# First cross attention of a two-block decoder: whole-chunk exponentials from four score banks, one work bank, and query transfers moved behind a barrier

## The reference

```python
# x: (16, 56, 128); ctx: (16, 1500, 96)
# block 0: 16 heads of width 8
q, k, v = split(x @ w_qkv + b_qkv)                     # self attention over 56 rows
x = layer_norm(x + mha(q, k, v) @ w_so + b_so)
qc = x @ w_q + b_q                                     # cross attention: 56 queries,
kc = ctx @ w_k + b_k                                   # 1500 keys per batch element
vc = ctx @ w_v + b_v
x = layer_norm(x + mha(qc, kc, vc) @ w_co + b_co)      # mha: softmax(q k^T / sqrt(8)) v
x = layer_norm(x + mlp(x))                             # 128 -> 512 -> 512 -> 128, relu
# block 1: 16 heads of width 64, cross attention over the same ctx, residual
```

## The kernel before

| stretch, us | what is done |
|---|---|
| 0 to 56 | loads, self attention of block 0 |
| 56 to 80.5 | the *query block*: projection, layer norm, queries of the cross attention |
| 80.5 to 444 | the *cross block*: first cross attention, one batch element after the other |
| 444 to 558 | the MLP and the folded weights of block 1 |
| 558 to 1077 | second cross attention |

## Time and profile before

### The profile page before, as it was taken

One profiled execution on the slowest core, in us unless ns is written; L12 is line 12 of the kernel. 1 busy time (PEld: TensorE's weight loads), 2 busy tenths in 40 slices (PEclk: granted clock), 3 DMA queues, 4 the chain that ended last, 5 costly groups with the idle time before them and its releaser, 6 DMA issues. The chain is left out here.

```text
span 1076.9 us, 31227 instructions
## 1 busy us (share of the span) xinstructions
PE 995.5 (92%) x11876; PEld 718.2 (67%) x11876; DVE 721.9 (67%) x1369; ACT 559.2 (52%) x1107; POOL 413.9 (38%) x290
## 2 busy tenths in 40 slices
PE   6947999999999999697879999999999999999997
PEld 3633666666667666555337777777777777777786
DVE  5738787777877786204776667676776776767752
ACT  2622777677767776522434545444444444444542
POOL 5613223322332223020015645545555454455542
PEclk8976999999999999889799999999999999999998
DMA  3515666775677652300111012111011111102100
GB/s 105 145 26 141 183 169 177 183 190 161 172 182 187 174 152 48 101 1 1 41 40 48 32 58 61 57 39 54 28 51 56 58 51 42 54 23 58 36 4 3
DMA packets 90924, 91.34 MB, mean 85 GB/s; under 512 B 50882, under 2 KB 77716, under 8 KB 90868
## 3 DMA queue, kind: packets, MB, share of 16 engines
q1 hardware_dynamic: 90868, 90.56, 30.7%
HBM read 51.15 MB, written 22.18 MB: 68 GB/s over the span
## 5 line engine op out<-in xcount | busy, mean ns | idle before, releaser
L1451 ACT ACTIVATE P<-PS 125x448 f32<-125x448 f32 x384 | 207.1, 544 | 265.2 <-PE PS L1360 263.3
L1341 POOL TENSOR_TENSOR Pl<-P 125x896 f16<-125x896 f32 x128 | 230.2, 1803 | 236.8 <-ACT P L1451 236.8
L1087 DVE TENSOR_REDUCE m<-PS 128x1 f32<-128x500 f32 x336 | 220.6, 674 | 115.8 <-PE PS L1078 113.8
L988 DVE TENSOR_REDUCE m_part<-PS 128x1 f32<-128x500 f32 x336 | 213.1, 673 | 58.5 <-PE PS L891 56.5
L966 ACT ACTIVATE Pb<-PS 125x448 f32<-125x448 f32 x384 | 184.6, 546 | 30.0 <-PE PS L864 28.6
L1376 PE MATMUL PS<-cNh,P 125*128 125x97 f16 x1344 | 197.9, 208 | 0.1
L1378 PE MATMUL PS<-cNh,Pl 125*128 125x97 f16 x1344 | 197.4, 207 | 0.0
L1377 PE MATMUL PS<-cNl,P 125*128 125x96 f16 x1344 | 196.8, 206 | 0.0
L891 PE MATMUL PS<-KH,Qmx 128*128 128x500 f16 x336 | 130.5, 390 | 21.3 <-DVE m_part L988 9.5
L1377 PEld LDWEIGHTS PS<-cNl,P 125*128 125x128 bf16 x1344 | 131.8, 98 | 25.5
L1376 PEld LDWEIGHTS PS<-cNh,P 125*128 125x128 bf16 x1344 | 131.1, 98 | 15.8 <-issue 3.2
(11 more groups left out here) (174 smaller groups left out, 1446.8 us busy)
## 6 DMA issues: line engine op xcount, KB each, us to landing
Kst<-k_halves SPq DMA_DIRECT2D x144, 125.0 KB, 2.9
k_halves<-KH SPq DMA_DIRECT2D x16, 750.0 KB, 3.3
cx<-in_ctx SPq DMA_DIRECT2D x16, 562.5 KB
d_cx<-in_ctx SPq DMA_DIRECT2D x16, 562.5 KB
c_halves<-cHi SPq DMA_DIRECT2D x16, 288.0 KB, 2.9
c_halves<-cLo SPq DMA_DIRECT2D x16, 288.0 KB, 7.8
cTh<-c_halves SPq DMA_DIRECT2D x16, 288.0 KB, 3.0
cTl<-c_halves SPq DMA_DIRECT2D x16, 288.0 KB, 4.0
```

The lines of the kernel that those rows point to most:

```text
L988: nc.vector.tensor_reduce(m_part[:, t, part:part + 1], PS[:, 6 + k % 2, 0:SP], AX.X, ALU.max).then_inc(s_reduced, 1)
L1087: nc.vector.tensor_reduce(m21[:, t, part:part + 1], PS[:, S1[k % 2], 0:SP], AX.X, ALU.max).then_inc(n_red, 1)
L1341: nc.gpsimd.tensor_tensor(Pl[:, c % NP], P1[:, c % NP], high, ALU.subtract).then_inc(n_low_p, 1)
L1451: nc.scalar.activation(P1[:, c % NP, half * HALF:(half + 1) * HALF], PS[0:KC, u % 3, 0:HALF], ACT.Exp).then_inc(n_exp, 1)
```

## The change

Nothing in the arithmetic changes. The parts are these:

- *Scores and exponentials.* Four banks (0 to 3) instead of three; a chunk takes two neighbouring banks, and one instruction of 896 columns makes its exponential. The scores of chunk c wait once, for the exponential of chunk c-2.
- *One work bank.* Keys, values, output, attention and the turned maxima all use bank 5. The maxima move there from bank 7, so piece 1 no longer waits until they are laid; every other user now waits for its forerunner.
- *Keys at every second step.* `k_piece` and `keep_keys` come at steps 5, 7 and 9 instead of 3, 4 and 5, `split_keys` at 6, 8 and 10. Steps 8 and 9 now have 1 and 2 pieces instead of 2 and 1, so the last piece comes after the last keys of step 9.
- *Output* at steps 3 and 4 instead of 6, 7 and 8.
- *Context.* Loads are cut into two halves and go a body further ahead; `round_rows` comes at step 12 for element b+4, in the starting body at step 0 for element 2 and at step 12 for element 3; `turn_rows` goes ahead of `lay_keys`.
- *Query block.* `norm_root` comes ahead of `keep_values`, the three value pieces have a bank each, and the 12 query transfers are the first thing that SP does in the cross block.

The diff, cut to its core:

```diff
-        OB, WB, WB2, MB = 4, 5, 3, 7
-        K_BANK, V_BANK = (WB2, WB, WB2), WB2
+        OB, WB = 4, 5
+        M_AT = slice(128, 256)
+        K_BANK, V_BANK = WB, WB
+        SCORE_BANKS = 4
...
-        BESIDE = beside(EARLY, (2, 2, 2, 2, 1, 2, 1, 2, 2, 1, 0, 0, 0, 0))
+        BESIDE = beside(EARLY, (2, 2, 2, 2, 1, 2, 1, 2, 1, 2, 0, 0, 0, 0))
+        K_AT = {5: 0, 7: 1, 9: 2}
...
+            if in_loop:
+                sp.wait_ge(v_made, (n - 2) * 3)
+            for half in range(2):
+                if in_loop and half == 1:
+                    sp.wait_ge(cx_low, n - 2)
+                sp.dma_start(cx[:, slot, 6 * half:6 * half + 6], ctx_768[n].rearrange("(p c) d -> p c d", c=NC)[:, 6 * half:6 * half + 6]).then_inc(cx_in[slot], 16)
...
-            elif k == 1:
-                wait_for(pe, att_kept, n - 3)
+                wait_for(pe, att_kept, n - 2)
             else:
-                pe.wait_ge(k_split, n * 3 + 1)
+                pe.wait_ge(k_split, n * 3 + k)
...
-            @block.sync
-            def _(sp):
-                sp.wait_ge(a_high, 1)
-...
...
             def _(act):
+                norm_root(act, a_var, a_root)
                 for k in range(NSP):
-                    keep_values(act, -1, 1, k)
-                norm_root(act, a_var, a_root)
+                    keep_values(act, -1, 1, k, early=True)
...
+                for block_row in range(2):
+                    for g in range(G):
+                        sp.dma_start(Q16[32 * block_row:32 * block_row + 32, g, :], Qall[32 * g:32 * g + 32, :]).then_inc(q_in, 16)
+                for g in range(G):
+                    sp.dma_start(Q16[64:96, g, :], Qrest[32 * g:32 * g + 32, :]).then_inc(q_in, 16)
+                load_context(sp, -1, 1, 3)
+
                 def body(i, par):
-                    if inside(i, par, 3):
-                        load_context(sp, i, par, 3)
+                    if inside(i, par, 4):
+                        load_context(sp, i, par, 4, in_loop=not (isinstance(i, int) and i < 0))
                     if inside(i, par, 2):
                         store_context(sp, i, par, 2)
-                        lay_keys(sp, i, par, 2, turn_next=inside(i, par, 3))
+                    if inside(i, par, 3):
...
+                        turn_rows(sp, i, par, 3)
+                    if inside(i, par, 2):
+                        lay_keys(sp, i, par, 2)
...
+                    wait_for(pe, exp_done, (n * NC + c - 1) * 2)
                     for half in range(2):
-                        u = 2 * c + half
-                        wait_for(pe, exp_done, n * 2 * NC + u - 2)
...
-                    if k == 1:
-                        wait_for(pe, m_laid, n)
...
-                    pe.matmul(PS[96:96 + MR, MB, 0:128], mneg[:], ident, start=True, stop=True).then_inc(m_turned, 1)
+                    if inside(i, par, 2):
+                        pe.wait_ge(k_split, n * 3 + 6)
+                    pe.matmul(PS[96:96 + MR, WB, M_AT], mneg[:], ident, start=True, stop=True).then_inc(m_turned, 1)
...
-                            nc.scalar.activation(Pb[:, c % NPB, half * HALF:(half + 1) * HALF], PS[0:KC, u % 3, 0:HALF],
-                                                 ACT.Exp, scale=SCALE0).then_inc(exp_done, 1)
-                        if c == 6 and inside(i, par, 3):
+                            nc.scalar.activation(Pb[:, c % NPB].rearrange("p (h c) -> p h c", h=2), PS[0:KC, banks:banks + 2, 0:HALF],
+                                                 ACT.Exp, scale=SCALE0).then_inc(exp_done, 2)
+                        if c == 0 and at_start:
                             round_rows(act, i, par, 3)
+                        if c == NC and inside(i, par, 4):
+                            round_rows(act, i, par, 4)
...
-                        if has_2 and 4 <= c < 7:
-                            split_keys(dve, i, par, c - 4)
+                        if has_2 and c - 1 in K_AT:
+                            split_keys(dve, i, par, K_AT[c - 1])
```

85 lines of the change are left out of this document (39 added, 46 removed).

## The result

The changed kernel takes 1084.22 us, the median of 12 runs (1083.46 to 1087.05); the kernel before took 1077.82 us (12 runs, 1075.36 to 1082.91). The ratio is 1.0058, with an interval of 1.0046 to 1.0070: slower, by 6.4 us. The profiled execution of the changed kernel has a span of 1084.9 us at a mean granted clock of 0.961; the one before had 1076.9 us at 0.963. What follows compares these two, 8.0 us apart; the execution after lies 2.6 us over the median of its kernel.

What follows compares the result with a forecast made beforehand. TensorE was taken to bound an element up to the maxima, a chain through VectorE behind them. Elements +9.1, element 14 +0.3, last -1.5, start +0.5 gave +8.4 us, predicted 1088 us (own range 1083 to 1094, whole range 1072 to 1097).

Steps and rivals of the forecast that it cites:

- Who ends an element: End of an element: TensorE waits 1.3 us for maxima behind last piece, reduction, third key split and `highest`; 3.57 us follow.
- +0.65 us an element: Elements with keys to make: each longer by 0.65 us, bounds -0.5 to +1.3, so +9.1 us over 14.
- Keys hand over with little over: Work bank: a keys piece frees it about 2.4 us from its start, the next user comes about 3 us later; hand-overs covered.
- the rival of +1.3: One work bank: its hand-overs show, +1.3 us an element, +17.5 us in all, 1098 us; chance 0.14.
- Freed scores win: Rival at the maxima: VectorE is through in time, each element gains 0.5 us, 1072 us in all; chance 0.20.
- Exponentials: ScalarE: a whole chunk takes 0.85 us back to back against 0.90 for halves; nothing gained in 14 elements.
- The last two elements: Element 14, without keys behind it, +0.3 us; the last, only scores and values, from 13.6 to 12.1 us, -1.5.
- The start: Query block to first scores: earlier first piece lost waiting for element 2's load, table load +0.8; +0.5 us in all.
- the rival of a kept start: Start: element 2's load lands at 84 us and 4 us stay won, 1084 us in all; chance 0.12.
- The sum: Whole kernel: 9.1 + 0.3 - 1.5 + 0.5 = +8.4 us on the profiled execution's 1078.86 us.

Runs made afterwards that it cites:

- Experiments 3 and 4: Changed kernel with maxima ahead of the third key split, in a score piece's bank (3: 1080.53 us); 4 also moves the late piece back to step 8 (1073.25 us).
- experiment 2: Changed kernel with one late piece moved back from step 9 to step 8, as before the change: 1090.44 us, ratio 1.0125 to the kernel before.
- experiment 5: Changed kernel with two exponentials of 448 columns for a chunk in place of one of 896, same four score banks: 1084.37 us, ratio 1.0057.
- experiment 1: Changed kernel with the load of element 2's context issued ahead of the 12 query transfers on SP: 1078.78 us, ratio 1.0009 to the kernel before.
- 9 and 11: Changed kernel with small plain copies in place of one of the two DMA transposes (9: 1088.35 us) or of both (11: 1084.29 us).

## Why the prediction was right

Predicted 1088 us, measured 1084.22: slower, inside the forecast's own range. Of the 3.8 us between them some 2.4 are the kernel before, which was taken at 1080.2 (mean of four times) and has a median of 1077.82 over 12. Its steps, one by one:

- *Who ends an element.* Right, with nearly every term. Predicted were: TensorE ready for the maxima at 17.6, last piece at 16.6, maxima turned at 18.94, a wait of 1.3 us, 3.57 us behind them. Measured in the element above: 258.60 - 1.22 - 239.83 = 17.55; 16.40; 18.77; 1.22; 3.56. Experiments 3 and 4 show both halves of the cause: the split on the chain (0.45 us) and then the late piece (0.30 us).
- *+0.65 us an element.* Measured +0.67. Over 14 elements 9.4 us, against 9.1.
- *Keys hand over with little over.* Right as a sum in the changed kernel (the rival of +1.3 did not come), but the cover was thinner than I wrote: experiment 2 pushes the keys 0.55 us late with one piece of 0.2 us moved.
- *Freed scores win.* The rival was wrong for the kernel as changed, and its size was wrong too. With both obstacles gone the maxima come 0.28 us sooner and the element is 0.09 us shorter, not 0.5: VectorE's split, which must go somewhere, moves behind the maxima.
- *Exponentials.* 0.917 us in the groups, 0.85 back to back (3.38 for four at 438.68), as taken. No gain in 14 elements: experiment 5, 22.51 against 22.54. The Trainium skill's formula (ScalarE: Activation LUTs, section What ACT_TABLE_LOAD costs) gives 932 ns for 896 columns, and 839 back to back; this trace agrees within 2% on both.
- *The last two elements.* Element 14: predicted +0.3, measured 0.0. The last: predicted -1.5, measured -0.5. The mis-sized term is ScalarE's saving: scores do wait for exponentials here (0.67 us at 439.65), and each starts only when four score matmuls are done. With halves in the same four banks the stretch takes 12.97 us (experiment 5), so the 0.5 us won come of the fourth bank and not of the longer instruction.
- *The start.* Predicted +0.5, as -0.3 for the maxima and +0.8 for the table. Predicted times were load out at 80.6, landed 87.9, keys split 89.7, maxima 97.9; measured 79.14, 86.84, 88.51, 96.80, all 1.1 to 1.5 us early, since the block ahead ended early: the first piece, put at 73.3, started at 71.70. That makes -1.4 for the maxima where -0.3 was predicted and the rival of a kept start had some -4. The table load stands where it was put, behind the first scores, but experiment 5, where it does not, shows it worth 0.2 us and not 0.8. The reason given, the order on SP's queue, is shown by experiment 1.
- *What I did not see.* The transposes now beside the context load, the late instruction fetch, the stop of 2.0 us and the lower clock behind it: (25.29 - 22.54) + (23.43 - 22.54) = 3.6 us in the profiled execution, 1.4 to 3.2 us in the traces of experiments 1 to 5, and 0.7 for the same two elements before. About half of the 3.6 is the lower clock: experiment 1, with a stop of 1.83 us and the clock high, pays 1.8. I had looked at the transposes' path only for a wait of their users, and none of these waits.

The sum was +8.4 us. Measured, by the same stretches: 9.4 for 14 elements at the steady difference, -1.1 because the first two show less of it, 3.0 for the stop (3.6 less 0.7), -1.4 for the start, -0.3 from the sixteenth laid maxima to the last output, and -1.6 behind the stage, where the diff changes nothing: the 8.0 between these two executions. By the medians it is 6.4. The mechanism of the main term is shown; that the sum comes out is in part luck: the start (2 us better), the first two elements (1 us) and the stages behind (1.6 us) made up for the stop that nobody foresaw (3 us) and the last element (1 us).

## What to carry to other kernels

When a change frees an engine at one point, follow the chain that ends the period with the new order written out, term by term: here the wait that was removed (0.5 us) was smaller than the one that the same edit built (1.3 us), and the busy shares of the engines showed neither. Two chains of nearly one length hide each other, so a repair that loses alone (the piece put back, +0.38 us) can win beside another (-0.30 us); try them together before dropping one. A load that everything waits for goes to the head of its queue, and where a large load stands right ahead of transposes by DMA, look at the instruction fetches; keeping the two apart is a repair that these runs suggest and none tried.

## What the runs showed of the hardware

- TensorE's instructions come as 16 KB packets in a DMA queue of their own: 128 waits more in its program moved them. With a load of 562 KB and a transpose by DMA issued 1 to 2 us apart, one fetch came 13.4 to 16.0 us behind its forerunner in place of some 10, and TensorE stopped for 1.4 to 2.7 us, for nothing else that the profile shows; with small copies in place of the transposes, or with a sixth of the load, there was no stop. In later passes of the loop there are no fetches, and no stops.
- In the profiled execution the granted clock fell to 1.2 GHz for 6.8 us behind that stop; the element behind it took 0.9 us more. In eight of the eleven traces with the stop it did not fall there.
- A transpose by DMA of the context's rows took 10.2 us to land beside the load and 6.8 beside a sixth of it.
- An exponential of 896 columns from PSUM takes 0.917 us; one of 448 takes 0.544; back to back it is 0.85 for the whole against 0.90 for two halves. The 2 us of busy time that the whole chunk saves ScalarE in an element changed nothing.
- A VectorE cast of 128 x 7 columns between two tiles in SBUF took 2.30 us, in place of 0.17, in the two runs (9 and 11) in which it started beside GpSimd's 2.36 us instruction of 1152 columns.
